# Cross attention heads packed two by two into the halves of TensorE's rows, and a new hand-written order

## What is computed

```python
x = x + _L0_attn_ref(_layernorm(x), gamma)            # softmax over -gamma*|yi-yj|^2, then attn @ y
x = x + _L0_xattn_ref(_layernorm(x), ctx_1024, ...)   # 16 heads, dk = 8, 154 keys, ALiBi slopes
x = x + _L0_ffn_ref(_layernorm(x), ...)               # router, top 2 of 8 experts by a 0/1 mask

scores = jnp.einsum('bhqd,bhkd->bhqk', q, k) / jnp.sqrt(jnp.float32(dk))
scores = scores + slopes[None, :, None, None] * dist[None, None, :, :]
attn = jax.nn.softmax(scores, axis=-1)
out = jnp.einsum('bse,ehd,bsd->bsh', mask, expert_w, hidden_states)
```

## Time and profile before

| what | value |
|---|---|
| median of 3 runs | 182.98 us (182.34 to 184.85) |
| span of the profiled execution | 182.3 us |
| PE busy, instructions | 173.4 us (95%), 1514 |
| DVE busy | 150.5 us (83%) |
| ACT busy | 105.8 us (58%) |
| POOL busy | 60.7 us (33%) |
| bytes read from and written to memory | 9.19 MB, 6.37 MB |

### The profile page before, as it was taken

The page is one execution under the profiler, slowest core; times in us unless marked ns, Lnnn a source line. Parts: engine busy times, 40 slices in busy tenths (PEclk is TensorE's granted clock), DMA queues, the critical chain, the costliest instruction groups (busy, mean ns, idle before and its releaser), DMA issues.

```text
span 182.3 us, 4382 instructions
## 1 busy us (share of the span) xinstructions
PE 173.4 (95%) x1514; PEld 123.6 (68%) x1514; DVE 150.5 (83%) x433; ACT 105.8 (58%) x219; POOL 60.7 (33%) x123
## 2 busy tenths in 40 slices
PE   6999999999899998999999999999997999999894
PEld 2355785477766685545465467775677969899893
DVE  7827879989999999998998998987299389699552
ACT  3036995979857396969789678979834040110100
POOL 4789733302363143855410002004397400010000
DMA  4930071636266554543742000001400010010002
GB/s 99 335 153 0 4 213 50 176 103 192 79 162 162 156 161 129 159 125 92 198 130 62 14 7 12 8 5 50 192 4 0 4 58 2 16 45 0 32 0 86
DMA packets 20003, 15.84 MB, mean 87 GB/s; under 512 B 1621, under 2 KB 18133, under 8 KB 19833
## 3 DMA queue, kind: packets, MB, share of 16 engines
q1 hardware_dynamic: 19982, 15.57, 29.1%
HBM read 9.19 MB, written 6.37 MB: 85 GB/s over the span
## 4 chain that ended last, share of the span: by engine, by line
PE 72%; DVE 19%; issue 3%; ACT 3%; POOL 1%; ACTq 0%; DVEq 0%
PE bank L1440 15%; DVE nm L1091 9%; PE bank L1371 8%; PE bank L1344 7%; PE bank L1316 6%; PE bank L1214 6%; PE bank L1263 6%; PE bank L1210 5%; PE bank L1279 4%; DVE y L989 3%; PE bank L1421 3%; PE bank L1340 2%; PE bank L1367 2%; ACT w L857 2%; PE bank L1390 2%
## 5 line engine op out<-in xcount | busy, mean ns | idle before, releaser
L1091 DVE TENSOR_REDUCE nm<-bank 128x3 f32<-128x462 f32 (+1 forms) x88 | 48.6, 614 | 0.8 <-PE bank L1316 0.6
L919 ACT ACTIVATE pt<-bank 128x512 f32<-128x512 f32 x80 | 43.3, 604 | 3.8 <-PE bank L1344 2.7
L1440 PE MATMUL bank<-ewT,ym 128*128 128x128 f32 x256 | 32.5, 277 | 0.0
L1440 PEld LDWEIGHTS bank<-ewT,ym 128*128 128x128 f32 x256 | 30.3, 192 | 0.2
L1316 PE MATMUL bank<-ks,qs 99*128 99x308 bf16 (+1 forms) x170 | 25.2, 262 | 0.0
L1344 PE MATMUL bank<-qs,ks 105*128 105x256 bf16 (+1 forms) x96 | 21.6, 309 | 0.0
L1316 PEld LDWEIGHTS bank<-ks,qs 99*128 99x128 bf16 x170 | 15.1, 98 | 8.3 <-DVE nm L1091 2.2
L1186 DVE TENSOR_TENSOR ym<-bank,y3T 128x512 f32<-128x512 f32 x24 | 15.1, 684 | 4.9 <-PE bank L1421 4.9
L798 POOL TENSOR_SCALAR ve<-mv 128x2 f32<-128x2 f32 (+1 forms) x6 | 1.3, 210 | 50.2 <-DVE mv L984 50.0
L1371 PE MATMUL bank<-pt,vm 128*32 128x256 f32 (+1 forms) x192 | 17.3, 456 | 0.0
L1263 PE MATMUL bank<-y1Tg,y1T 128*128 128x512 f32 x32 | 16.6, 601 | 0.3 <-ACT y1Tg L837 0.3
(11 more groups left out here) (143 smaller groups left out, 287.8 us busy)
## 6 DMA issues: line engine op xcount, KB each, us to landing
ks<-k_scratch SPq DMA_DIRECT2D x4, 480.0 KB, 4.5
q_scratch<-qpart SPq DMA_DIRECT2D x8, 192.0 KB, 2.1
qs<-q_scratch SPq DMA_DIRECT2D x8, 192.0 KB, 3.4
xs<-in_x_dram SPq DMA_DIRECT2D x4, 256.0 KB, 4.2
q_scratch<-qpart SPq DMA_DIRECT2D x8, 128.0 KB, 2.4
qs<-q_scratch SPq DMA_DIRECT2D x8, 128.0 KB, 3.1
...
```

Of the source, the lines that this page charges most:

```text
L919: nc.scalar.activation(pt[:, n % RING, :], at("scores", b, i)[:, :], ACT.Exp).then_inc(exps, 1)
L1091: v.tensor_reduce(nm[b][:, n:n + heads], at("maxima", b, g)[:, 0:heads * J].rearrange("p (s j) -> p s j", s=heads), AX.X, ALU.max, negate= ...
L1440: last = mm(at("experts", b, p)[:, tile(t)], ym[:, e, tile(t)], ewT[:, e, :], start=False, stop=(e == E - 1), skip_group_check=True)
```

## The change

Each head gets its own 54 rows (48 products, 3 for ALiBi, 3 for its maxima) in one half of TensorE's rows: `place(h)` says in which half `s` (partitions 0 to 53, or 64 to 117) and at which place `a`. Two heads of different halves are issued alternately and write different banks.

- `maxima`: three pairs of heads in two neighbouring banks, six matmuls of 154 columns (256 in all, before 86 of 308 and 84 of 154), one VectorE maximum over both banks (128x924 elements); 46 groups instead of 88.
- `scores`: two items at once in two banks (40 steps on TensorE; ScalarE still takes 80).
- Keys need no zeroed copies: `keys` on ScalarE and VectorE works on 308 instead of 616 columns, and the keys' way through memory moves half the bytes. But every DMA of k_rows, q_rows, qout, qin, kout, kin and min is now two, one for each half: 159 DMAs instead of 102.
- All lists of ORDER and TURNS are new; WARM has 19 idle matmuls instead of 44.

```diff
-AUG = 2 * ROWS
+AUG = DK * COPY
 MAXROW = AUG + 3
-TOP = MAXROW + 6
+TOP = MAXROW + 3
...
-        x:0.0 gamma:0.0 x:1.0 x:2.0 k_rows:0.0 cols:0.0 x:3.0 context:0.0 weights:0.0 experts:0.0 k_rows:1.0
+        cols:0.0 experts:0.0 x:0.0 x:1.0 x:2.0 weights:0.0 gamma:0.0 k_rows:0.0 q_rows:0.0 k_rows:1.0 x:3.0
...
-    "y1T:0.0": 28, "sqT:0.0": 4, "probs:0.0": 2, "y1T:3.0": 3, "maxima:0.0": 2, "probs:3.0": 4,
-    "scores:0.0": 1,
+    "y1T:0.0": 17, "scores:1.2": 2,
...
+def place(h):
+    return h // (2 * G) * G + h % G, h // G % 2
...
             def qin(b, k):
...
-                load(qs[b][2 * DK * r:2 * DK * (r + n), :, c],
-                     q_scratch[b][r:r + n, :, c].rearrange("k (r a) n -> (k r) a n", a=PAIRS), qs_in[b])
+                for s in range(2):
+                    load(qs[b][HALF * s + DK * r:HALF * s + DK * (r + n), :, c],
+                         q_scratch[b][s, r:r + n, :, c].rearrange("k (r a) n -> (k r) a n", a=PAIRS), qs_in[b])
...
             def maxima(b, g):        # VectorE
...
-                v.tensor_reduce(nm[b][:, n:n + heads],
-                                at("maxima", b, g)[:, 0:heads * J].rearrange("p (s j) -> p s j", s=heads),
+                for s in range(2):
+                    dve.wait_ge(a_ps[s], groups_to(b) + g + 1)
+                v.tensor_reduce(nm[b][:, :, n:n + heads],
+                                both("maxima", b, g)[:, :, 0:heads * J].rearrange("p s (n j) -> p s n j", n=heads),
                                 AX.X, ALU.max, negate=True).then_inc(maxed, 1)
...
             def maxima(b, g):        # TensorE
...
-                for a, t, s, heads in pieces(b, g):
-                    last = mm(at("maxima", b, g)[:, at_ * J:(at_ + heads) * J], qs[b][0:MAXROW, a, tile(t)],
-                              ks[b][0:MAXROW, a, s:s + heads, 0:J], start=True, stop=True)
+                for i in range(min(GROUP, entries(b) - n)):
+                    a, t = (n + i) // n_t, n_t * p + (n + i) % n_t
+                    for s in range(2):
+                        rows = slice(HALF * s, HALF * s + MAXROW)
+                        last[s] = mm(at("maxima", b, g, s)[:, i * J:(i + 1) * J], qs[b][rows, a, tile(t)],
+                                     ks[b // 2][rows, a, b % 2, 0:J], start=True, stop=True)
...
-            def scores(b, i):
-                turn("scores", b, i)
+            def scores(b, q):
+                for s in range(2):
+                    turn("scores", b, 2 * q + s)
...
-                        last = mm(bank_[:, :], ks[b][0:TOP, h // 2, h % 2, 0:JM], qs[b][0:TOP, h // 2, c], start=True,
-                                  stop=True)
+                                last[s] = mm(bank_[:, :], ks[b // 2][rows, a, b % 2, 0:JM], qs[b][rows, a, c],
+                                             start=True, stop=True)
```

More of the change, by code:

```diff
@@ L95 @@
[L95 to L98 removed]
+        table:0.0 y1T:0.0 sqT:0.0 dist:0.0 dist:0.1 dist:0.2 dist:0.3 soft:0.0 keys:0.0 keys:0.1 probs:0.0 soft:0.1
+        soft:0.2 probs:0.1 y1T:1.0 probs:0.2 soft:0.3 sqT:1.0 sqT:2.0 probs:0.3 y2T:0.0 dist:1.0 query:0.0 y1T:2.0
@@ L99 @@
+        scores:3.18 scores:3.19 values:3.2 values:3.3 mask:2.0 mask:2.1 y3T:3.0 aoT:3.1 y3T:3.1 mask:3.0 mask:3.1
     """,
     "vector": """
[L101 to L104 removed]
@@ L167 @@
-        experts:3.5 experts:3.6 spread:3.6 experts:3.7 experts:3.8 experts:3.9 spread:3.7 experts:3.10
-        experts:3.11 experts:3.12 experts:3.13 experts:3.14 experts:3.15
+        start:0.0 y1T:0.0 sqT:0.0 dist:0.0 dist:0.1 dist:0.2 dist:0.3 keys:0.0 keys:0.1 key_values:0.0 probs:0.0
+        tail_values:0.0 y1T:1.0 self:0.0 probs:0.1 sqT:1.0 sqT:2.0 probs:0.2 self:0.1 self:0.2 probs:0.3 sqT:3.0
+        dist:1.0 self:0.3 y2T:0.0 dist:1.1 query:0.0 dist:1.2 y1T:2.0 dist:1.3 dist:2.0 y2T:0.1 dist:2.1 query:0.1
@@ new lines @@
+        maxima:2.10 values:1.2 scores:1.7 maxima:2.11 scores:1.8 scores:1.9 wo:0.0 mT:2.1 values:1.3 maxima:3.0
+        maxima:3.1 scores:2.0 divide:1.0 values:1.4 scores:2.1 values:2.0 divide:1.1 scores:2.2 values:2.1 scores:2.3
+        scores:2.4 maxima:3.2 values:2.2 y3T:0.0 aoT:1.0 maxima:3.3 maxima:3.4 route:0.0 maxima:3.5 scores:2.5
+        values:2.3 values:2.4 scores:2.6 maxima:3.6 scores:2.7 mT:3.0 wo:1.0 scores:2.8 scores:2.9 divide:2.0
+        values:2.5 values:2.6 divide:2.1 mask:0.0 maxima:3.7 values:2.7 values:2.8 values:2.9 scores:3.0 scores:3.1
@@ new lines @@
+        scores:3.2 scores:3.3 aoT:2.0 values:3.0 divide:2.2 wo:2.0 divide:2.3 values:3.1 scores:3.4 maxima:3.8
+        values:3.2 values:3.3 maxima:3.9 maxima:3.10 maxima:3.11 values:3.4 experts:0.0 experts:0.1 aoT:2.1 divide:3.0
+        divide:3.1 experts:0.2 wo:2.1 mT:3.1 aoT:3.0 experts:0.3 wo:3.0 experts:0.4 y3T:1.0 experts:0.5 route:1.0
+        scores:3.5 scores:3.6 scores:3.7 y3T:2.0 y3T:2.1 experts:0.6 experts:0.7 route:2.0 mask:1.0 scores:3.8
+        scores:3.9 values:3.5 values:3.6 spread:1.0 spread:1.1 mask:2.0 values:3.7 values:3.8 values:3.9 divide:3.2
@@ L174 @@
     """
-        y1T:0.0 vp:0.0 sqT:3.0 maxima:0.4 maxima:0.9 dist:3.1 maxima:0.18 self:2.1 maxima:1.1 query:2.1
-        scores:0.2 scores:0.6 scores:0.9 maxima:1.18 maxima:1.21 mT:1.0 maxima:2.3 maxima:2.7 scores:1.1
-        maxima:2.15 scores:1.8 scores:1.13 scores:1.15 maxima:3.4 divide:1.0 maxima:3.12 mT:3.0 maxima:3.14
-        scores:2.12 divide:2.1 mT:3.1 scores:3.4 scores:3.8 y3T:1.0 route:1.0 y3T:2.0 spread:1.0 spread:1.5
-        route:2.1 mask:2.1 spread:2.5 mask:3.0 spread:3.5
-    """,
@@ L221 @@
[L221 to L227 removed]
+        y1T:0.0 dist:0.2 vp:0.0 probs:1.2 maxima:0.0 maxima:0.2 dist:3.0 dist:3.2 maxima:1.0 maxima:1.3
@@ new lines @@
+    """,
+    """
+        sqT:2.0 query:0.0 y1T:2.0 dist:2.3 y2T:1.1 query:1.1 maxima:0.6 maxima:0.8 maxima:0.10 y2T:2.1
+        maxima:1.2 scores:0.1 scores:0.4 scores:0.11 pv:0.1 maxima:2.6 maxima:2.7 maxima:2.9 maxima:2.10
+        maxima:2.11 scores:1.18 scores:2.1 scores:2.3 scores:2.7 aoT:1.0 scores:2.11 scores:2.15 mask:0.0
+        scores:3.5 maxima:3.8 maxima:3.11 divide:3.0 mT:3.1 y3T:1.0 scores:3.11 route:2.0 spread:1.0
+        experts:1.0 aoT:3.1 experts:2.0 mask:3.1 spread:3.3
+    """,
@@ new lines @@
+    """
+        probs:0.2 sqT:3.0 probs:1.1 self:1.1 y2T:1.0 query:1.0 probs:2.2 maxima:0.6 maxima:0.8 maxima:0.10
+        mT:0.0 maxima:1.2 scores:0.3 scores:0.9 y2T:3.1 scores:0.13 scores:0.17 mT:1.0 query:3.1 maxima:2.6
+        maxima:2.7 maxima:2.9 maxima:2.10 maxima:2.11 scores:1.19 divide:1.0 scores:2.6 y3T:0.0 route:0.0
+        scores:2.19 scores:3.4 maxima:3.8 maxima:3.11 divide:3.1 aoT:3.0 scores:3.10 y3T:2.1 scores:3.18
+        spread:1.7 divide:3.3 spread:2.4 experts:2.1 spread:3.2
```

425 lines of the change are left out of this document (193 added, 232 removed).

## The result

The changed kernel takes 207.16 us (median of 4 runs, 207.15 to 214.69), the kernel before 183.03: a ratio of 1.129 (95% interval 1.122 to 1.137). It is 24 us slower, where 178.4 us was forecast and 172 to 187 was the range.

The account below looks back on a forecast made before the run. It took TensorE and VectorE, both full, to bound the middle, and TensorE alone the tail. Span 182.3 +4.1 (start) +0 +2.3 (middle) +1 (queue) -12 (tail) = 177.7, with 0.7 outside the span 178.4 us; range 172 to 187.

Parts of the forecast that it names:

- middle: First maxima on VectorE to the end of mcat:3.1: TensorE's sum +2.0, VectorE's near it, +2.3 us taken.
- queue: SP's DMA queue: batch 2's maxima wait for the remainder of its queries' 24 DMAs, +1 us (0 to 3.5).
- tail: From mT:3.1 to the end: TensorE loses 13.2 us of work, 1.2 given back, -12 us.
- start: Up to the first dist matmuls: later gamma +2.1 us, lower clock level +2, together +4.1 (0 to 7).
- start and queue cost in full: Rival: +6.5 us at the start and +3.5 at maxima:2.0, 183.3 us, no change; chance 0.14.
- groups at 0.20: Lower bound of the middle: each group of maxima matmuls takes 0.20 us instead of 0.25, giving -0.7 us.
- the 1.2 us given back for `y3`: Tail: y3 and route fall beside GpSimd's select, TensorE waits for masks, 1.2 us (0 to 3).
- Dear changes of shape: Rival on TensorE's order: a switch costs more than 0.10 us; at 0.2 in all, 189 us; chance 0.13.
- serial halves: Rival: half-row matmuls don't run beside each other, score pairs 0.44 us, 193 us; chance 0.05 together with serial loads.
- serial loads: Rival: 98 ns loads in series, 0.59 us a maxima group, +15.6, 194 us; chance 0.05 together with serial halves.

Follow-up runs that it names:

- e10: The change without the queries' way through memory, each query buffer filled once with constant rows: 190.32 us, ratio 1.044.
- e4: The kernel before with each DMA of kout, qout and qin divided into two of half the partitions: 205.44 us, ratio 1.125.
- e12: The change with projection columns reordered so both halves write in one DMA, parts two and three read together, earlier start, new SP order: 185.82 us, ratio 1.019.
- e15: e12 with GpSimd's select held back until the last mcat and three experts pieces moved behind mT:3.1: 184.95 us, ratio 1.015.
- e13: e10 with each VectorE maximum reading only 77 of a head's 154 columns: 186.05 us, ratio 1.014.

## Why the prediction was wrong, step by step

The terms of the sum against what the traces show (spans; "without queries" is e10 less the kernel before):

| term | predicted | without queries | with them |
|---|---|---|---|
| to `dist:0.0` | +2.1 | +3.0 | +2.9 |
| `dist:0.0` to first maxima (clock at the start, step order) | +2 + 0 | +2.9 | +9.9 |
| middle | +2.3 | +12.9 | +24.7 |
| queue | +1 | left out | +17.1, within the rows above: 7.0 and 11.8, less 1.6 in the tail and 0.1 at the start |
| tail | -12 | -12.8 | -14.4 |

Of the 27.7 us by which the span missed its forecast (205.4 for 177.7), 16.0 are the queue's and 10.6 the middle's; the start and the way to the first maxima add 1.9 and the tail takes off 0.8.

**The queue.** The step that failed is "24x0.5+2.1+3.4 = 17.5 us from query:2.0", with "+1 (0 to 3.5)". It priced one batch's way, on its own, and not the queue. The trace of the kernel before says otherwise: an issue of 0.56 us and 57 more DMAs give 32 us of SP's time on top of 50.9, most of it within the 66 us in which queries went out (29.5 to 95.7). Even that is too little: 39 us were added, since the issue of a half is longer (0.61 us for a write, 0.68 for a read, medians, where 0.5 was taken). In a queue in strict order these come one after the other: batch 0's queries stood behind 16 issues for keys, batch 1's behind batch 0's, and batch 2's maxima behind all of batch 3's queries. The prediction looked at batch 2 alone, where the wait was 2.9 us and so within its range; the larger waits were those of batches 0 and 1, 7.8 and 4.5 us. Term +1, measured 17 (205.4-188.4); e4 shows a cost of the same kind, +22 us, on the kernel before, by the divided DMAs alone. The rival "start and queue cost in full" had the right kind of cost, at `maxima:2.0` alone, and a price of 3.5 us. The Trainium skill (page "DMA: Bandwidth & Descriptors", section "Issuing engines are not separate DMA queues") calls the sequencer's time to start a DMA usually small beside the DMA. Here a write's 0.64 us stood beside a landing of 2.1 to 2.3 us, but DMA after DMA the issues were a third of the chain, so the measurement decides. The Trainium skill (page "SBUF — State Buffer", section "Can I just issue two DMAs to hit both halves?") says that two transfers, one on each half of the partitions, serialize, and that only one transfer over all 128 partitions reaches all ports. e4 and e12 agree that the one transfer is the cheaper, by the time of its issues; what the ports add is not shown here.

**The start.** Gamma was scaled at 9.82 us (8.9 and the upper 10.2 had been worked out from the earlier trace rows), `dist:0.0` started at 15.34 (14.5). The clock did what was forecast; TensorE's first rows of the changed kernel:

```profile
1.55 5.43 PE L1205 MATMUL banks<-idle 128*128 128x512 bf16 x17 [1.55 <-DVE idle L967]
12.77 1.15 PE L1244 MATMUL banks<-ident,y 128*128 128x128 f32 x4 [5.80 <-DVE y L984]
...
15.34 2.02 PE L1258 MATMUL banks<-y1Tg,y1T 128*128 128x512 f32 x2
...
17.58 1.46 PE L1258 MATMUL banks<-y1Tg,y1T 128*128 128x512 f32 x2
...
19.09 1.02 PE L1258 MATMUL banks<-y1Tg,y1T 128*128 128x512 f32 x2
```

The idle matmuls end at 7 us, TensorE stands for 5.8 us, the first tile of `dist` takes 2.02 us, the second 1.46 and the third 1.02: less than two tiles at the lower level, not four. +6.0 us up to the first maxima without queries, +4.1 predicted, and 0 to 7 was the range. About right.

**The middle.** The prices were right or a little high, by the rows of e12: 0.21 us a group (0.25 taken), 0.23 a pair, 0.10 a change of shape. A VectorE maximum over 924 columns is shown 1.11 us long, with the next start 1.03 behind (1.03 forecast). From the first maxima to `mT:3.1` the trace has 27 changes of shape before and 96 after, as counted. The Trainium skill's rule (page "TensorEngine Tiling (Array Packing)", section "Tiling Modes") that a change of tiling mode drains TensorE agrees in so far as the trace shows a cost each time, also for half rows: 0.10 us. What failed is the step from prices to time: "TensorE's sum is +2.0, VectorE's is near it, and I take +2.3" lets two engines that are both full work beside each other without waits. Before, they did: TensorE was idle 1.5 us of the middle (74.14-72.63), at 5 places. In e12, with the queue out of the way, it is idle 7.75 us (86.50-78.75) and stands 19 times ahead of a matmul. Its busy time holds waits as well, since a matmul is shown at its full length, 0.28 us on average, where nothing follows it. An estimate from the starts of the two traces puts a number on it: if each matmul is priced by the shortest distance to the next start that its kind commonly shows, changes of shape included, TensorE's own work in the middle is 69 us before and 70 to 71 in e12, and the time above that 5 and 16 us. So of the 12.4 us by which e12's middle is longer, some 1.5 are work, for +2.0 by the prices, and some 11 are waits, where the prediction allowed 0.3.

Where these waits come from is known in part. The three steps slowed by GpSimd are 2.8 us of the middle (e15), of which at most 0.9 reach the end. Of the 12 stands that are longer than 0.15 us (5.9 us), 7 were for VectorE to read out maxima (2.5 us) and 2 for DMAs (2.6), and e13 says that VectorE's maxima are worth 3.5 us of the middle. Which of the rest the new order makes necessary and which the pairing of heads stays open: no run has the one without the other.

One bound of the prediction does not follow from its prices: groups at 0.20 take some 2.1 us off the middle, which makes it about 0 and not -0.7.

**The tail.** -12 predicted, -12.8 without queries, -14.4 with them; the sum of moved and cheaper steps was right, and its 13.2 before the 1.2 us given back for `y3` is nearer still. GpSimd's `select` did collide with VectorE, as was feared by the earlier trace rows, but the place was another: it slowed the last `mcat`, ahead of the mark, and not `y3` (four normalisations took 1.08 us in the change).

**The rivals.** Dear changes of shape, serial halves and serial loads are all excluded by the rows above. Slower had a chance of 0.18, all of it by mechanisms that did not occur; the kernel is slower by a cause that was written down as a term of 1 us, and by one that was not written down, the waits of two full engines for each other.
